# A graph attention loop on one core: the weighted sum of a step comes ahead of the second half of the query expansion on TensorE

## The reference

```python
h = relu(layernorm(x))
q, k, v = h@wq+bq, h@wk+bk, h@wv+bv
scores = sum(q[dst]*k[src], -1)/16 + edge_weight*we + be
attn = softmax of scores over the edges of each dst
out = segment_sum(v[src]*attn, dst)
y = layernorm(h + out + h@ws+bs)*g1+b1
y = layernorm(y + gelu(y@w_ff1+b_ff1)@w_ff2+b_ff2)*g2+b2
return x + y
```

## Time and profile before

| | us |
|---|---|
| runs (3) | 2398.57, 2402.55, 2403.62; median 2402.55 |
| profiled execution, its own time | 2402.3 |
| its span, first to last instruction | 2400.5 |
| TensorE busy in the span | 2212.3 (92%) |
| VectorE, GpSimd, ACT busy | 1757.4 (73%), 1653.7 (69%), 1168.5 (49%) |
| mean granted clock of TensorE | 0.982 |

### The profile page before, as it was taken

How to read it: one execution, slowest core, us unless ns; L and a number is a source line. 1 busy time by engine, 2 the same in 40 slices (tenths; PEclk the granted TensorE clock), 3 DMA queues, 4 the chain that set the end, 5 groups by cost and what they waited for, 6 DMA issues and landing times. The chain is left out here.

```text
span 2400.5 us, 69609 instructions
## 1 busy us (share of the span) xinstructions
PE 2212.3 (92%) x14709; PEld 1867.1 (78%) x14710; DVE 1757.4 (73%) x7359; ACT 1168.5 (49%) x2903; POOL 1653.7 (69%) x1828
## 2 busy tenths in 40 slices
PE   6789889898999999999999999999999999989995
PEld 4678767776777777877887888888888888877884
DVE  7668667676777777777777777777778888774378
ACT  5545444444444444444444544555445555454454
POOL 4747777777777777777777777777777777402356
PEclk8989999999999999999999999999999999989997
DMA  8344444444444444444444444444444444350014
GB/s 266 103 116 139 137 138 136 137 138 137 139 137 137 136 137 138 138 138 139 136 138 137 137 138 136 138 135 137 137 140 136 139 140 137 89 159 0 0 53 135
DMA packets 148118, 311.09 MB, mean 130 GB/s; under 512 B 33550, under 2 KB 84609, under 8 KB 148088
## 3 DMA queue, kind: packets, MB, share of 16 engines
q0 software_dynamic: 75264, 205.62, 29.7%
q1 hardware_dynamic: 54702, 90.19, 11.7%
q10 hardware_dynamic: 18122, 14.96, 2.0%
HBM read 290.21 MB, written 20.43 MB: 129 GB/s over the span
## 5 line engine op out<-in xcount | busy, mean ns | idle before, releaser
L831 POOL DMA_INDIRECT work<-h_rows,idx x1536 | 1461.4, 951 | 483.2 <-issue 445.4
L919 PE MATMUL bank<-work 128*128 x3520 | 836.5, 380 | 0.0
L1010 DVE SCALAR_TENSOR_TENSOR work<-bank,work 128x257 bf16<-128x257 f32 x1764 | 646.7, 424 | 231.7 <-SPq L795 200.3
L856 PE MATMUL bank<-q,onehot 128*128 x5304 | 740.2, 274 | 70.2 <-DVE work L1010 52.7
L919 PEld LDWEIGHTS bank<-work 128*128 128x128 f32 x3520 | 634.6, 190 | 78.9
L856 PEld LDWEIGHTS bank<-q,onehot 128*128 128x128 bf16 x5304 | 510.2, 98 | 154.6 <-issue 92.6
L967 ACT COPY work<-bank 128x256 f32<-128x256 f32 x880 | 285.5, 377 | 397.5 <-PE bank L906 395.0
L963 ACT ACTIVATE work<-work 128x1 f32<-128x1 f32 x440 | 129.6, 295 | 624.5 <-DVE work L1076 624.5
L1076 DVE CUSTOM_DVE_ANT_0 work<-bank,work 128x512 f32<-128x512 f32 x440 | 329.8, 750 | 108.7 <-PE bank L862 77.1
L964 ACT ACTIVATE work<-work 128x512 f32<-128x512 f32 x440 | 311.6, 708 | 0.0
L906 PE MATMUL bank<-ident,work 128*128 128x128 f32 x1760 | 266.7, 274 | 29.0 <-ACT work L964 29.0
(11 more groups left out here) (192 smaller groups left out, 1601.7 us busy)
## 6 DMA issues: line engine op xcount, KB each, us to landing
dst_words<-dst_short SPq DMA_DIRECT2D x99, 512.0 KB
work<-h_rows,idx POOLq DMA_INDIRECT x1568
bias<-h_rows ACTq DMA_DIRECT2D x56, 128.0 KB
r_rows<-bias ACTq DMA_DIRECT2D x55, 128.0 KB
work<-r_rows SPq DMA_DIRECT2D x49, 128.0 KB, 2.1
acc<-in_x SPq DMA_DIRECT2D x4, 1536.0 KB, 15.7
h_rows<-acc SPq DMA_DIRECT2D x12, 512.0 KB, 6.7
work<-in_x SPq DMA_DIRECT2D x12, 512.0 KB, 3.9
```

The lines of the kernel that those rows point to most:

```text
L831: pool.indirect_dma_start(rows[:, u, j, 0:D], None, h_rows, bass.IndirectOffsetOnAxis(idx[:, half, u * J + j:u * J + j + 1], 0)).then_inc( ...
L856: last = nc.tensor.matmul(banks[j][:, 0:D1], onehot[:, k, j, :], q3[:, bass.ds(b, 1), c, 0:D1], start=(c == 0), stop=(c == 2))
L919: last = nc.tensor.matmul(banks[6 + k][:, 0:D1], probs[:, j, :], rows[:, bass.ds(slot, 1), j, :], start=(j == 2), stop=(j == 1))
L1010: last = nc.vector.scalar_tensor_tensor(out=product[:, j, 0:D1], in0=banks[j][:, 0:D1], scalar=SCALE, in1=rows[:, bass.ds(slot, 1), j, :], ...
```

## The change

In TensorE's iteration the four matmuls of the weighted sum of step `s` come ahead of the second half of the expansion for step `s + 2`, and with that half goes its wait for `dotted`. No instruction is added or removed, and the other engines' code is the same.

```diff
                         pe.wait_ge(scored, s + 2)
                         pe.wait_ge(probs_done, s * 2 + 1)
                         spread_scores(1 - k)
-                        pe.wait_ge(dotted, s * 2 + 4)
-                        expand_q(k, 1, b)
                         for j in (2, 3, 0, 1):
                             if j == 0:
                                 pe.wait_ge(probs_done, s * 2 + 2)
                             last = nc.tensor.matmul(banks[6 + k][:, 0:D1], probs[:, j, :], rows[:, bass.ds(slot, 1), j, :], start=(j == 2), stop=(j == 1))
                         last.then_inc(summed, 1)
+                        pe.wait_ge(dotted, s * 2 + 4)
+                        expand_q(k, 1, b)
                         if steps == U and u == 2:
                             turn_h(pe.snap(pe.to_reg(r * NW + i), min_val=0, max_val=B * NW))
```

## The result

The changed kernel takes 2510.91 us (median of 4 runs, 2508.71 to 2512.28), the kernel before 2401.61 us (2398.57 to 2403.62). The ratio is 1.0455, with a 95% interval of 1.0437 to 1.0474: 109 us slower. The forecast was 2462 in a range of 2430 to 2515. Direction and mechanism hold, and the loss is 1.8 times the forecast's: the time lies inside the range, but above the 2506 us at which the forecast's own part of it ended. The profiled execution has a span of 2506.9 us.

A forecast was written before the change was run, and what follows sets the result against it. Gathers were taken to bound most of the loop, TensorE's steps the last part. A trip of 33.44 + 2.92 = 36.36 us, 4.55 per step, gave +60 us on 2402: 2462 us, range 2430 to 2515.

The forecast's parts named there:

- What bounds the kernel: Whole loop: gathers set most of the time at 5.0 us per chunk, TensorE's step time of 4.18 us the last part.
- Nothing gained by the removed wait, a little by the early slot: Weighted sum in TensorE: removed wait gains 0; gathers, freed a slot sooner, start at most 1.5 us earlier.
- The ring: Spread, weighted sum, second half expansion, second dots, score, next spread: 4.41 us per plain step, up 0.47 from 3.94.
- load step: Step with the register load: 4.62 us before, growing by 0.36 as the score's lead over the spread shrinks.
- T: TensorE's transposes of the probabilities: with their exponentials they put the next spread at 4.14 us at worst, not setting the step.
- second pair to score 0.92 us: VectorE, second pair of dots to score: 0.92 us, taken from the trace before and used in the 4.37 us spread start.
- Two dots cover some 0.8 us, so I take nothing: VectorE's register work behind the second pair: up to 0.73 us might come out; nothing charged, 0.2 us for the range.
- rival 3: VectorE's register work comes out behind the two dots: 4.7 us per plain step, +125 us, 2527 us; chance 0.12.
- The forecast's upper bound: High case with 0.2 us for register work: 4.6 us per plain step, 4.69 mean, +104 us.
- The share that the gathers hide: Early loop: gathers keep the pace until shortly before 1100 us; from there 233 steps go at 4.55 us.
- The clock: TensorE's clock: nothing charged for 0.47 us new idle per step; rival of a falling clock, 2600 us at worst, chance 0.02.
- Rivals 1 and 2: Not slower: (1) expansion isn't late, 2401 us; (2) gathers hide the longer step, 2402 us; together chance 0.10.

The follow-up runs named there:

- The split sum: Changed kernel with the second half of the expansion behind two of the weighted sum's four matmuls: 2404.62 us, ratio 1.0009; a plain step took 3.97 us.
- the run with 36.42 us: Changed kernel with VectorE's register work moved between the two pairs of dots, except at u = 0: 2462.89 us, ratio 1.0265.
- the step of 5.56 us: Step behind the register load in the changed kernel with register work moved between the pairs of dots in all steps: 2483.72 us, ratio 1.0338.

## Why the prediction was right, and where its size was off

**What bounds the kernel**: right. The runs with three gathers show both halves of it: early steps fall to 4.17 us without the fourth gather, and the mean of all, 4.19, is what late steps took before (4.18).

**Nothing gained by the removed wait, a little by the early slot**: right. The first gather that waits for a slot starts at 140.20 us instead of 141.44, with 21.3 us of waiting in place of 22.2, and no part of the time shows it, as the gathers no longer set the end.

**The ring**: right in every link but one. Forecast against measured: sum to expansion 1.74 and 1.74, expansion to third dot 0.97 and 0.97, score to spread 0.30 and 0.29, project_h step 4.92 and 4.97, load step 4.98 and 4.99. T and the exponentials don't set it in plain steps. The split sum shows that it is a ring with a threshold.

**The step that failed** is "second pair to score 0.92 us", and with it "Two dots cover some 0.8 us, so I take nothing". That row was taken from a step in which VectorE had four dots in a row. In the changed kernel the wait for the expansion also holds back the register instructions that stand behind it in VectorE's queue. Third dot to score is 1.02 us in plain steps and 1.34 in two steps of a trip, where more register work stands there. Those are 0.10 us in each of four steps and 0.42 and 0.37 in two (in the second the spread ahead hadn't waited, so its follower wasn't late). With project_h's 0.05 and 0.01 of the load step a trip is 37.61 us, not 36.36. Of these 1.25 us the run with the register work moved takes back 1.19, and 48 of the 49 us by which the forecast fell short. This was rival 3, given 0.12, in a milder form: 0.10 in plain steps and 0.42 in two, instead of 0.29 in all. The forecast's upper bound, 4.6 per plain step and 4.69 in the mean, has the mean that came (4.70), but by luck: plain steps are 4.51 and two steps 0.3 longer. Its sum from there was +104 us; the measured loss is 109.

**The share that the gathers hide**: right in kind. The forecast had them set the pace up to about 1100 us; at 4.70 us per step they set it nowhere: every trip takes 37.6 to 37.7 us, the early ones too. The excess of 1.25 us in 55 trips makes 69 us, of which 49 are seen, because a kernel with the forecast's trip does wait for gathers: in the run with 36.42 us, early trips take up to 39.9 us.

**The clock**: right. It is 1.00 in all four windows after, with TensorE idle for 0.35 us or more ahead of the spread in five steps of eight. The Trainium skill (TensorE: Matmul & The Clock Gate, "A second HAM failure mode") tells of a kernel in which frequent small idle times between groups of matmuls made the clock swing; this trace doesn't agree.

Rivals 1 and 2 are out by the two waits and by the gathers' 140.6 us of waiting for slots.

## What to carry to other kernels

When work moves on one engine, close the ring through the others: start to start from the moved result to its reader, on to what that reader releases, and back. Whatever is longest, that ring or the engine's own work, is the new step. A duration between two rows holds only for the wait that stood ahead of them then: where a new wait comes ahead, everything that the engine's sequencer did behind it in hidden time may come out. It can be moved ahead of the new wait, but only in steps where that wait is there; elsewhere the move itself costs time, as the step of 5.56 us shows. And ask in which stretch something else sets the pace: here the gathers hid half of what the order costs.

## What the hardware showed that was not expected

The same kernel of before took 2400 to 2402 us in three groups of runs and 3328 and 3278 us in two, once under the chip number that later gave 2400. In those two, engines stood still for up to 9.4 us at a time (3.4 in the mean of the row shown), with no engine's row to release them. VectorE's register instructions, of which the page shows nothing as busy, were worth 0.1 to 0.4 us a step once they had only two dots to hide behind, and 0.65 us where they stood between the two pairs of a late VectorE.
